# A decoder layer in float32: how the products of convolved pairs and queries are laid out and summed

## The reference, cut to what matters

```python
def _L0_xattn_ref(k, v, q, ssm_kernel, D, head_dim):
    kv = jnp.einsum('bhil,bhjl->bijhl', k_, v_)          # 8 x 8 pairs of channels per head
    kv_f = jnp.fft.rfft(kv, n=fft_size)
    kernel_f = jnp.fft.rfft(ssm_kernel, n=fft_size)
    y = jnp.fft.irfft(kv_f * kernel_f, n=fft_size)[..., :L]
    out = y + kv * D[None, None, None, :, None]
    out = jnp.einsum('bijhl,bhil->bjhl', out, q_)        # sum over the 8 channels i of each j
    ...
x = x + _L0_xattn_ref(ctx_2048, ctx_2048, _layernorm(x, axis=-1), ssm_kernel, D, 8)
```

## Time and profile before

| | |
|---|---|
| median of 3 runs | 1149.06 us (1146.43 to 1155.12) |
| the profiled execution | 1150.28 us, of which 1148.5 us span |
| mean granted TensorE clock | 0.932 of full |
| busy, TensorE matmul | 972.9 us (85% of the span) |
| busy, VectorE | 632.7 us (55%) |
| busy, GpSimd | 429.1 us (37%) |
| busy, ScalarE | 256.4 us (22%) |
| the stage of the change | 337.2 to 516.8 us |

### The profile page before, as it was taken

The page is one execution under the profiler, slowest core; times in us unless marked ns, Lnnn a source line. Parts: engine busy times, 40 slices in busy tenths (PEclk is TensorE's granted clock), DMA queues, the critical chain, the costliest instruction groups (busy, mean ns, idle before and its releaser), DMA issues. The chain is left out here.

```text
span 1148.5 us, 14772 instructions
## 1 busy us (share of the span) xinstructions
PE 972.9 (85%) x4721; PEld 663.7 (58%) x4721; DVE 632.7 (55%) x1362; ACT 256.4 (22%) x787; POOL 429.1 (37%) x354
## 2 busy tenths in 40 slices
PE   3697989979879999977999989999797979797961
PEld 2365555656566666657744347767474746574740
DVE  3787786876369999997499943212222222221210
ACT  1282552825331111111311002111111111111100
POOL 2344260432336666643015023343434343443322
PEclk9798999989899999995899999999898989898986
DMA  7200000002043233302304037989797979887943
GB/s 273 75 1 1 0 0 0 0 1 65 1 156 110 80 83 85 87 1 92 129 0 165 37 120 223 262 244 258 200 264 193 250 203 243 222 266 200 259 96 46
DMA packets 44686, 143.18 MB, mean 125 GB/s; under 512 B 7345, under 2 KB 11697, under 8 KB 35697
## 3 DMA queue, kind: packets, MB, share of 16 engines
q1 hardware_dynamic: 25392, 91.35, 23.2%
q0 software_dynamic: 15488, 37.76, 17.5%
q10 hardware_dynamic: 3776, 13.70, 3.1%
HBM read 114.36 MB, written 28.43 MB: 124 GB/s over the span
## 5 line engine op out<-in xcount | busy, mean ns | idle before, releaser
L1236 PE MATMUL ps<-arena 128*128 128x128 f32 (+3 forms) x2560 | 632.1, 402 | 77.1 <-DVE arena L1178 53.8
L1236 PEld LDWEIGHTS ps<-arena 128*128 128x128 f32 x2560 | 403.1, 194 | 255.0 <-issue 149.5
L526 POOL DMA_INDIRECT out<-arena,scatter_rows x64 | 100.6, 1572 | 238.1 <-DMA out<-arena,scatter_rows 176.9
L1192 DVE COPY scatter_rows<-slot_rows_u 128x1 uint32 (+1 forms) x64 | 9.8, 154 | 313.1 <-POOLq L525 234.2
L1236 PE MATMUL ps<-features_T,arena 128*128 (+2 forms) x640 | 115.1, 338 | 0.0
L431 POOL TENSOR_TENSOR arena<-arena 128x512 f32<-128x512 f32 x48 | 49.2, 1053 | 164.6 <-DVE arena L773 164.5
L571 ACT ACTIVATE arena<-ps 128x512 f32<-128x512 f32 (+2 forms) x148 | 82.1, 573 | 123.2 <-DVE residual L1144 61.2
L1236 PEld LDWEIGHTS ps<-features_T,arena 128*128 128x128 f32 x640 | 83.9, 192 | 37.3 <-issue 37.3
L515 POOL DMA_INDIRECT arena<-token_rows,gather_rows x64 | 65.2, 1018 | 71.9 <-DVE gather_rows L1171 52.7
L581 ACT ACTIVATE arena<-arena 128x128 f32<-128x128 f32 x192 | 74.0, 387 | 66.1 <-DVE arena L761 66.1
L738 ACT ACTIVATE arena<-ps 128x256 f32<-128x256 f32 x64 | 24.5, 383 | 285.4 <-PE ps L1236 257.7
(11 more groups left out here) (160 smaller groups left out, 999.0 us busy)
## 6 DMA issues: line engine op xcount, KB each, us to landing
arena<-wexp SPq DMA_DIRECT2D x64, 1024.0 KB
arena<-toeplitz_rows SPq DMA_DIRECT2D x32, 256.0 KB, 3.1
arena<-ctxE SPq DMA_DIRECT2D x32, 192.0 KB, 3.3
residual<-x SPq DMA_DIRECT2D x4, 1024.0 KB, 5.8
token_rows<-arena SPq DMA_DIRECT2D x16, 256.0 KB, 2.0
arena<-suT ACTq DMA_DIRECT2D x1, 2048.0 KB, 7.8
arena<-sdT ACTq DMA_DIRECT2D x1, 2048.0 KB, 12.7
out<-residual ACTq DMA_DIRECT2D x1, 2048.0 KB, 7.6
```

Of the source, the lines that this page charges most:

```text
L526: pool.indirect_dma_start(out, bass.IndirectOffsetOnAxis(ap=idxs[:, s % 2:s % 2 + 1], axis=0), ysb[:, s % 2, :], None, compute_op=ALU.add) ...
L1236: ins = TE.matmul(out_ap, lhsT, rhs, start=(n == 0), stop=(n == len(pairs) - 1))
```

## The change

The addends get a new layout, in which the channel j and not the addend k is innermost.

- `direct[m, d, j]` takes y[8 d + j] · q[j + d] for d = 0 to 3 in one instruction of 1024 elements (L948 after), with the four overlapping windows of q given by one access pattern. It writes contiguously.
- `parts[m, 88]` has 88 words a group. Words 0 to 47 are three rows of 16, one for each of d = 1, 2, 3: the eight products y[8 d + i] · q[i] are written from word d of its row on (L951, 768 elements, in runs of 8), so that word j of the row and word j + 8 are the two pieces that belong to channel j; the rest of the row is zero. Words 64 to 71 take the eight products of distance 4 (L954, 256 elements).
- `half_sums` on GpSimd now does all 32 groups: it adds the four rows of `direct` by pairs into words 72 to 87 (512 elements, two runs of 16), and the first two shifted rows, 12 words each, into words 48 to 59 (384 elements).
- `head_sums` is one reduction over the seven rows of 8 in words 32 to 87, that is over elements 8 words apart: 32·8 outputs, 1792 elements read. It waits for GpSimd's half sums.
- The words 0 to 63 of both buffers are cleared once by GpSimd (L482, 4096 elements) ahead of the loop; VectorE waits for that (`pads_ready`).
- TensorE writes the eight batches of a bank 64 words apart and no longer 36, so that one access pattern can walk over all 32 groups.
- `wring` and what follows it move by 640 words.

```diff
--- before.py
+++ after.py
@@ -99,6 +99,7 @@
         AREA = 34400
         arena = sb("arena", [P, AREA])
         place = [0]
+        WRING_AT = 17536
 
         def carve(shape, at=None, rows=P):
             n = int(np.prod(shape))
@@ -154,14 +155,15 @@
         O2 = carve([DC, B, S])
         kvb = carve([NTR, DC * B, NPAIR], at=11904)
         qx = carve([NTR, DC * B, 12])
-        prodb = carve([2, DC * B, 8, 8])
-        halfsum = carve([2, 2 * B, 8, 4])
-        assert place[0] <= 25088
+        direct = carve([2, DC * B, 4, SD])
+        parts = carve([2, DC * B, 88])
+        shifted, half_rows = parts[:, :, :, 0:48], parts[:, :, :, 32:88].rearrange("p s m (k j) -> p s m j k", j=SD)
+        assert place[0] <= WRING_AT + 8192
 
         oeven = carve([NT // 2, D], at=11904)
 
         NW = 4
-        wring = carve([NW, 2048], at=16896)
+        wring = carve([NW, 2048], at=WRING_AT)
         suT = carve([DC, SHD])
         sdT = carve([SHD // P, D])
         gwT = carve([DC, E])
@@ -180,7 +182,7 @@
         g2 = carve([NT, 8])
         m8 = carve([NT, 8])
         cnt = carve([NT])
-        assert place[0] <= 16896, place[0]
+        assert place[0] <= WRING_AT, place[0]
 
         sel = carve([NT // 2, 2, E], at=8192)
 
@@ -238,6 +240,7 @@
         conv_filled = [sem(f"head_slot{k}_multiplied") for k in range(NTR)]
         conv_used = [sem(f"head_slot{k}_products_taken") for k in range(NTR)]
         half_ready = sem("head_half_sums_ready")
+        pads_ready = sem("shifted_rows_cleared")
         conv_done = sem("heads_convolved")
         even_added = sem("even_tiles_added")
         stats3_ready = sem("ln3_stats_ready")
@@ -466,15 +469,17 @@
 
             def half_sums(s, i):
                 pool.wait_ge(conv_used[s], i + 2)
-                pv = prodb[:, s % 2, 2 * B:, :, :].rearrange("p m j k -> p (m j) k")
-                G.tensor_tensor(halfsum[:, s % 2].rearrange("p m j k -> p (m j) k"), pv[:, :, 0:4], pv[:, :, 4:8],
-                                ALU.add).then_inc(half_ready, 1)
+                rows = parts[:, s % 2]
+                G.tensor_tensor(rows[:, :, 72:88].rearrange("p m (d j) -> p m d j", d=2), direct[:, s % 2, :, 0:2, :],
+                                direct[:, s % 2, :, 2:4, :], ALU.add)
+                G.tensor_tensor(rows[:, :, 48:60], rows[:, :, 0:12], rows[:, :, 16:28], ALU.add).then_inc(half_ready, 1)
 
             pair_products(0, 0)
             pair_products(1, 0)
 
             pool.wait_ge(stats2_ready, 1)
             G.tensor_tensor(rstd[:], rstd[:], minus_half[:], ALU.pow).then_inc(rstd2_ready, 1)
+            G.memset(parts[:, :, :, 0:64].rearrange("p s m k -> p (s m) k"), 0.0).then_inc(pads_ready, 1)
             last = SH // NTR - 1
             with pool.Fori(0, last) as i:
                 for s in range(NTR):
@@ -938,30 +943,25 @@
                 dve.wait_ge(qx_ready, i * NTR + s + 1)
 
                 dve.wait_ge(conv_done, i * NTR + s + 1)
-                y = ps[:, 4 * (s % 2):4 * (s % 2) + DC, 0:B * NPAIR].rearrange("p l (b n) -> p l b n", n=NPAIR)
-                q = qx[:, s, :, :].rearrange("p (l b) j -> p l b j", l=DC)
-                pr = prodb[:, s % 2].rearrange("p (l b) j k -> p l b j k", l=DC)
-                for d in range(4):
-
-                    V.tensor_tensor(pr[:, :, :, :, d], y[:, :, :, 8 * d:8 * d + 8], q[:, :, :, d:d + 8], ALU.mult)
-                    if d:
-
-                        V.tensor_tensor(pr[:, :, :, d:8, 3 + d], y[:, :, :, 8 * d:8 * d + 8 - d],
-                                        q[:, :, :, 0:8 - d], ALU.mult)
-                        V.tensor_tensor(pr[:, :, :, 0:d, 3 + d], y[:, :, :, 8 * d + 8 - d:8 * d + 8],
-                                        q[:, :, :, 8 - d:8], ALU.mult)
-                V.tensor_tensor(pr[:, :, :, 0:4, 7], y[:, :, :, 32:36], q[:, :, :, 4:8], ALU.mult)
-                V.tensor_tensor(pr[:, :, :, 4:8, 7], y[:, :, :, 32:36], q[:, :, :, 0:4], ALU.mult)\
-                 .then_inc(conv_used[s], 1)
+                y = ps[:, 4 * (s % 2):4 * (s % 2) + DC, :].rearrange("p l (b n) -> p (l b) n", n=64)
+                q = qx[:, s, :, :]
+                V.tensor_tensor(direct[:, s % 2], y[:, :, 0:4 * SD].rearrange("p m (d j) -> p m d j", d=4),
+                                bass.AP(q.tensor, q.offset, [list(q.ap[0]), [12, DC * B], [1, 4], [1, SD]]), ALU.mult)
+                sh = shifted[:, s % 2]
+                V.tensor_tensor(bass.AP(sh.tensor, sh.offset + 1, [list(sh.ap[0]), [88, DC * B], [17, 3], [1, SD]]),
+                                y[:, :, SD:4 * SD].rearrange("p m (d j) -> p m d j", d=3),
+                                q[:, :, 0:SD].unsqueeze(2).broadcast_to((P, DC * B, 3, SD)), ALU.mult)
+                V.tensor_tensor(parts[:, s % 2, :, 64:72].rearrange("p m (h j) -> p m h j", h=2),
+                                y[:, :, 4 * SD:NPAIR].unsqueeze(2).broadcast_to((P, DC * B, 2, 4)),
+                                q[:, :, 4:12].rearrange("p m (h j) -> p m h j", h=2), ALU.mult).then_inc(conv_used[s], 1)
 
             def head_sums(s, i):
 
-                dve.wait_ge(conv_used[s], i + 2)
+                dve.wait_ge(half_ready, i * NTR + s + 1)
                 o = O2.rearrange("p l b s -> p (l b) s")[:, :, ds((i * NTR + s) * SD, SD)]
-                V.tensor_reduce(o[:, 0:2 * B, :], prodb[:, s % 2, 0:2 * B], axis=AX.X, op=ALU.add)
-                dve.wait_ge(half_ready, i * NTR + s + 1)
-                V.tensor_reduce(o[:, 2 * B:, :], halfsum[:, s % 2], axis=AX.X, op=ALU.add).then_inc(conv_done, 1)
-
+                V.tensor_reduce(o, half_rows[:, s % 2], axis=AX.X, op=ALU.add).then_inc(conv_done, 1)
+
+            dve.wait_ge(pads_ready, 1)
             head_products(0, 0)
             last = SH // NTR - 1
             with dve.Fori(0, last) as i:
@@ -1372,9 +1372,8 @@
 
                 pe.wait_ge(conv_used[(s + 2) % NTR], i + (s // 2 + 1))
                 for lt in range(DC):
-                    ins = product(ps[:, 4 * (s % 2) + lt, 0:B * NPAIR],
-                                  [(tring[:, s, (lt - mt) * P:(lt - mt + 1) * P],
-                                    kvb[:, s, mt * B:(mt + 1) * B, :].rearrange("p b n -> p (b n)"))
+                    ins = product(ps[:, 4 * (s % 2) + lt, :].rearrange("p (b n) -> p b n", n=64)[:, :, 0:NPAIR],
+                                  [(tring[:, s, (lt - mt) * P:(lt - mt + 1) * P], kvb[:, s, mt * B:(mt + 1) * B, :])
                                    for mt in range(lt + 1)])
                 ins.then_inc(conv_filled[s], 1)
```

## The result

| | before | after |
|---|---|---|
| median of 20 runs each | 1150.5 us | 1158.94 us |
| range | 1144.07 to 1156.45 | 1148.32 to 1165.36 |
| ratio | | 1.0065, 95% interval 1.0042 to 1.0088 |
| the profiled execution | 1150.28 us, span 1148.5 | 1163.25 us, span 1161.4 |

The changed kernel is slower by 0.65%, 5 to 10 us: within 1%, and on the side of slower. The two profiled executions differ by 12.9 us of span, more than the medians do, because each is one draw from a spread of 12 us (before) and 17 us (after).

What follows compares the result with a forecast made beforehand. The prediction took VectorE to bound the loop: products 2.31, reduction 3.19 and fixed part with wait 0.25 make 5.75 us a head against 5.61, +4.5 us over 32 heads. That gave 1154.8 profiled, 1153.5 as median, range 1120 to 1168.

Steps and rivals of the forecast that it cites:

- What bounds the stage: Loop over 32 heads: VectorE sets the pace at 5.61 us a head; TensorE is the next bound at 4.79.
- The products: VectorE's products of a head: contiguous writes at 1.05 ns an element instead of 1.78, 3.72 to 2.31 us, saving 1.41.
- The odd starts of the shifted rows: Product runs beginning at an odd word: bounds 1.05 and 1.78 ns an element; 1.05 taken, as runs are 8 long.
- The sum: VectorE's one reduction over 1792 elements, read 8 words apart: 1.78 ns each, 3.19 us plus 0.25 fixed part and wait.
- Rival A: VectorE's reduction: hopping read nearly free, TensorE becomes the bound at 4.79 us a head, 1122.8 us; chance 0.25.
- rival C: VectorE's reduction: hopping read costs more than the write, 2.51 ns an element, 7.06 us a head, 1195.5 us; chance 0.17.
- The rule of two adjacent words on an 8-byte boundary: VectorE streams: full rate only in such runs; one hopping source costs 1.73 ns, destination 1.71, or 2.50 at 24 words' step.
- VectorE's sum, times 32: VectorE in the loop: 2.31 + 3.19 + 0.25 = 5.75 us a head against 5.61, +0.14, times 32 +4.5 us.
- The clearing at nothing: GpSimd's memset of 4096 elements ahead of the loop: 3.5 us, hidden, with 11 us in hand on VectorE's side.
- Nothing else moves: Outside the loop: SP and ScalarE do nothing new, other stages only have arrays at new places; no cost.
- Rivals D: GpSimd becomes the bound in the loop if half sums cost more, 6.05 us a head, +14, 1163 us; chance 0.04.
- rival E: TensorE writes PSUM with gaps more slowly; at 1.5 times 7.19 us a head, +50.6, 1199.7 us; chance 0.03.

Runs made afterwards that it cites:

- before_writes_contiguous: Kernel before, its 12 products a head writing channels next to each other, half sums and reductions reading as before (wrong assignment of addends); ratio 0.9789 to before.
- write_steps: Probe in the changed kernel: first product writes at steps of 1, 4, 2 and 256 words in the four slots; 1225, 1993, 692 and 1055 ns, total not timed.
- sum_contiguous: Changed kernel, its reduction reading the same 56 words of a group in contiguous order (wrong assignment of addends); ratio 0.9795 to before.
- in the second: Changed kernel measured again without edit, beside its variants, against the kernel before: 1156.89 against 1154.88 us, ratio 1.0031.
- before_psum_64: Kernel before, only with TensorE writing the batches of a PSUM bank 64 words apart and VectorE reading them there; ratio 0.9992 to before.

## Why the prediction was right or wrong, point by point

- **What bounds the stage**: right. VectorE before and after; in the experiments that relieved it, TensorE at 4.84 us a head (4.79 foreseen).
- **The products**: right in size, and in part in the cause. 2.34 us measured, 2.31 forecast. That the write's step costs is shown (before_writes_contiguous, write_steps), but the prediction laid the 1.78 ns to it nearly alone; of the saving of 1.38 us it made 0.79, and the other 0.59 came from nine instructions fewer. The odd starts of the shifted rows, which I could not read from a row, are free (L951: 0.87 us for 768, 0.86 forecast).
- **The sum**: right. 3.50 us with its wait against 3.44. The step that carried the forecast, that a read which hops by 8 words pays what the write paid, holds for long instructions: 0.77 ns an element at the read (step 8, sum_contiguous), 0.75 at the write (step 4, write_steps). Rival A (free) and rival C (twice) both fall with it. The rule of two adjacent words on an 8-byte boundary, which the prediction took from the Trainium skill ("Vector Engine (DVE) Microarchitecture Reference", section Measured stream behaviour on trn2), is not borne out as it stands: with a step of 2 no two words are adjacent, and read (2.01 us) and write (692 ns) ran at the full rate. No run had the step of 24 words to which the 2.50 belongs.
- **VectorE's sum, times 32**: +0.14 a head forecast. From the first product to the first L999 the stage grew from 180.7 to 188.8, +8.1 us or 0.25 a head. 5.84 against 5.62 between two reductions gives +0.22; of the 0.11 missed, 0.06 is in the reduction (3.50 against 3.44) and 0.03 in the products. The other 1.1 us of the stage are two single waits of VectorE that the kernel before does not have, at the second head for TensorE and at the loop's last turn:

```profile
346.40 1.22 DVE L948 TENSOR_TENSOR arena<-ps,arena 128x1024 f32<-128x1024 f32 x1 [0.64 <-PE ps L1236]
...
510.27 1.23 DVE L948 TENSOR_TENSOR arena<-ps,arena 128x1024 f32<-128x1024 f32 x1 [0.54 <-DVE arena L962]
```

- **The clearing at nothing**: wrong. The step that failed is "Cost nothing, with 11 us in hand on VectorE's side": I looked for who waits for the memset and for what is queued behind it on GpSimd, not for what runs beside it on VectorE. It costs 3.1 us (entry 20.8 to 21.0 in the six traces of kernels that have it, 17.8 without in most, 18.8 in one, 18.0 with the clearing on VectorE). The Trainium skill ("SBUF — State Buffer", section Who interferes with whom) states the rule: GpSimd and VectorE share a pair of ports, which a tensor_scalar in a two-port mode and a GpSimd instruction take in turn and hold for the whole instruction. This trace agrees: 3.70 us, ending 0.3 us behind the memset. That this tensor_scalar runs in such a mode is not shown, but fits its pace, 0.47 us from start to start for 512 elements (ten in 4.79 us in the kernel before), where L999 takes 0.59.
- **Nothing else moves**: wrong. "The other stages only have arrays at new places" left TensorE's clock out. Behind the stage 7.0 us came back, reproducibly, because TensorE did six more tiles at full clock. Why it does so in this kernel stays open. I had the clock of the stage in the rows and not that of the stretch behind it.
- **The total**: +4.5 us forecast from one term; the traces have +8.1 and +3.1 lost and −7.0 regained, +4.3. That the forecast came out so near is luck: two terms that I did not have (+3.1, −7.0) and one that was too small (+8.1 for +4.5) nearly cancel. The medians say +8.4 in the first comparison and +2.0 in the second, within the range given; why the first shows more than the traces is not known.
- **Rivals D and E**: GpSimd stayed 1.34 us a head short of work, with 4.5 us busy as worked out (4.47); TensorE's bursts kept 5.1 us. The rule that rival E took from the Trainium skill ("PSUM — Partial Sum Buffer", Specifications), that a non-contiguous pattern slows matmuls, does not show for runs of 36 words with gaps of 28: 5.09 us for the 20 matmuls in before_psum_64.

## What to carry to other kernels

When a layout is turned so that the writes become contiguous, the reads take the stride over. Price both sides per element, and the instructions beside them: 14 instructions became four here, and what that gave (0.59 us a head in the products) went to a hop that cost more on the read (1.39 us) than on the write (0.79). Look for a layout in which each side touches at least two words of the same 16 bytes in a row, the rule with which the steps measured here agree (pairs of the output index innermost, the summed index next), which serves both. And for every instruction added to an idle GpSimd, ask which VectorE instruction runs at that moment.

## What the runs showed of the hardware that I had not expected

- A VectorE reduction reads at full rate with a step of 2 words (2.01 us for 1792 elements) and pays the whole surcharge from 4 words on (3.43; 3.40 for 8). At 16 words it is 2.37 us for 1280.
- A GpSimd memset, which reads nothing, holds up a VectorE tensor_scalar that starts beside it for its full length: 3.70 us instead of 0.54. With the memset on VectorE the entry is 3 us shorter.
- Small losses ahead of a stage in which TensorE starts from the low clock need not reach the end. The stage of before (180.7 us), followed by the same work, had 45.3, 40.6 or 39.4 us behind it, and where a kernel was traced more than once its value repeated (45.3 three times, 38.3 twice).
